# An attention and mixture-of-experts layer: one-hot token lists and gathers by token in place of a sorted copy of the rows

## The chip, the cores and the metric

The kernel runs on 1 core of one Trainium2 chip. The metric is the device time of one execution in microseconds; the median of 3 runs of the kernel before is 584.5 us (583.47 to 586.1). A page and a trace of one profiled execution go with it; that execution took 583.73 us.

## The reference

Two sublayers on x of 16 x 112 = 1792 tokens of 256 numbers, all in float32:

```
x = x + attention(layernorm(x), ctx, mask)       # 16 heads of 16, 375 context rows
flat = layernorm(x)                               # 1792 x 256
probs = softmax(flat @ router_w)                  # 8 experts
w, idx = top_k(probs, 2);  w = w / sum(w)
h = silu(einsum('td,edf->etf', flat, w1))         # w1: 8 x 256 x 512
y = einsum('etf,efd->etd', h, w2)                 # w2: 8 x 512 x 256
x = x + einsum('td,te->td', y, cw)                # cw: w of the two chosen experts, else 0
```

Only two of eight experts count for a token, so both kernels compute 1792 x 2 = 3584 rows of expert work and not 8 x 1792.

## The kernel before, in words

Each engine has its own instruction stream, written out by hand, and they meet at semaphores. Matmuls take operands in a rounded format (float32r); to keep float32 accuracy every operand is split in a high part and a low part (raw minus high), and a product is three matmuls (high x high, low x high, high x low).

**Attention** (lines 346 to 355, 721 to 745, 942 to 958, 1281 to 1383) is untouched by the change but for a few instructions on GpSimd behind line 554. It ends at about 310 us of the span.

**Residual, second norm, routing.** `project_output` (PE) and `residual` (DVE) make x2, 14 tiles of 128 tokens; `all_rstd` and `normalise_rows` make xn2, its layer norm. `flat_transpose`, `route` and `logits_back` give the logits, tokens on partitions. `find_first` and `find_second` (DVE, lines 1028 to 1046) mark the two chosen experts of each token in 0/1 tiles of 128 x 14 x 8. `rank` (PE, 1420) counts with a triangular matrix how many earlier tokens chose the same expert. `place_rows` (DVE, 1048) turns that into the place of each of the 3584 rows in a list sorted by expert, where each expert starts at a multiple of 256 (`TG`); `plan_steps` (1070) lists the expert of each of the 21 steps (`STEPS`), `weigh` (1078) the two weights of each token.

**Dispatch.** SyncE has filled `sorted_x`, a DRAM tensor of 21 x 256 rows, with zeros (line 420). When the places are known GpSimd scatters the rows of xn2 into it by 28 indirect DMAs of 128 rows (line 587). SyncE waits for all of them (461) before it loads the first block of rows.

**Experts**, 21 steps of 256 sorted rows, software pipelined; a hardware loop (`Fori`) runs steps 3 on in pairs. In turn t PE does `hidden(t)` (24 matmuls of 256 columns), `rows_transpose(t+1)` (4 transposes), `expert_out(t-1)` (24 matmuls). ScalarE: `w1_high(t+1)`, the write of y to `sorted_y` in DRAM, `rows_high(t+1)`, `silu(t)` (two passes). VectorE: `rows_low(t+1)`, `h_low(t)`, `copy_y(t-1)`, `w2_high(t+1)`. GpSimd: the low parts of w1 and w2 (line 592). SyncE loads w1, w2 (512 KB each) and 256 rows per step. Buffers are double.

**Combine.** When every step's y is in `sorted_y`, GpSimd gathers it back by token, 28 indirect DMAs of 128 rows (line 614); VectorE multiplies by the weight and adds to x2 (line 1165); SyncE writes out in 7 DMAs (473).

## Time and profile before

| | |
|---|---|
| median of 3 runs | 584.5 us (583.47 to 586.1) |
| profiled execution | 583.73 us, its span 582.0 us |
| busy in the span | PE 434.5, weight loads 383.9, VectorE 375.2, ScalarE 231.3, GpSimd 263.9 us |
| mean granted clock of TensorE | 0.873 |
| DMA | 93.00 MB, 160 GB/s |

The same in 40 slices of 14.55 us, each digit the busy share in tenths:

```
PE   3557799999999999999987472005999999998000
DVE  3765657777777777777735855001999999996233
ACT  3321235555555555555561130002545545553000
POOL 7352412222222222222006003774798999895574
PEclk9787769999999999999998685556999999999655
DMA  8979499999999999997245502426678878862354
```

PE is TensorE, DVE VectorE, ACT ScalarE, POOL GpSimd. Slices 0 to 20 are attention, 21 to 23 the second norm and the routing, 24 to 26 the dispatch, 27 to 36 the experts, 37 to 39 the combine.

### The profile page before, as it was taken

Reading aid. Unit: us, or ns where it says so; the run is one execution under the profiler, and the core shown is the slowest. Engines: PE = TensorE matmul, PEld = TensorE weight load, DVE = VectorE, ACT = ScalarE, POOL = GpSimd, SP = SyncE. Lnnn points to the kernel's source line nnn. Section 1 sums busy time; section 2 is a strip of 40 time slices with the busy share of each in tenths; the row PEclk is TensorE's granted clock in tenths of the full one; section 3 lists DMA queues with packets and bytes.
Section 4 is the critical chain, followed back from the end, with each engine's and each line's share of the span. In section 5 each row is a group of like instructions: output and inputs, shape, how many; then the busy total and the mean of one; then the engine's idle time right before and its main releaser. Section 6 shows DMA issues by size and latency. Waiting matters only on the chain.

```text
span 582.0 us, 10906 instructions
## 1 busy us (share of the span) xinstructions
PE 434.5 (75%) x4123; PEld 383.9 (66%) x4123; DVE 375.2 (64%) x733; ACT 231.3 (40%) x296; POOL 263.9 (45%) x170
## 2 busy tenths in 40 slices
PE   3557799999999999999987472005999999998000
PEld 2445588888888888888767462004999999998000
DVE  3765657777777777777735855001999999996233
ACT  3321235555555555555561130002545545553000
POOL 7352412222222222222006003774798999895574
PEclk9787769999999999999998685556999999999655
DMA  8979499999999999997245502426678878862354
GB/s 187 188 187 243 166 146 124 145 144 144 146 143 147 146 143 147 144 148 104 34 129 179 201 1 82 170 99 193 192 232 260 239 250 246 241 214 91 108 155 133
DMA packets 82504, 93.00 MB, mean 160 GB/s; under 512 B 19824, under 2 KB 75280, under 8 KB 82464
## 3 DMA queue, kind: packets, MB, share of 16 engines
q1 hardware_dynamic: 74064, 79.61, 64.6%
q0 software_dynamic: 2688, 7.34, 3.9%
q10 hardware_dynamic: 5712, 5.51, 2.8%
q8 instruction: 27, 0.44, 0.4%
q14 instruction: 13, 0.11, 0.1%
HBM read 51.58 MB, written 22.14 MB: 127 GB/s over the span
## 4 chain that ended last, share of the span: by engine, by line
PE 46%; issue 21%; DVE 14%; ACT 8%; POOL 5%; DMA 3%; ACTq 2%; SPq 1%; DVEq 0%; POOLq 0%
PE ps L1178 17%; PE ps L1228 10%; PE ps L1243 7%; PE ps L1257 7%; POOL chosen_rows L614 4%; ACT h_hi L775 3%; ACT h_f L774 2%; DVE y_out L1112 2%; DVE k_f L827 2%; ACTq L779 1%; DVE neg_max L843 1%; PE ps L1270 1%; DVE h_lo L1105 1%; DVE x_rows_sb L890 1%; PE ps L1399 1%
## 5 line engine op out<-in xcount | busy, mean ns | idle before, releaser
L843 DVE TENSOR_REDUCE neg_max<-ps 112x1 f32<-112x376 f32 x256 | 132.8, 545 | 48.7 <-PE ps L1228 44.8
L592 POOL TENSOR_TENSOR w_lo<-w_raw,w_hi 128x1024 fp32r<-128x1024 f32 x42 | 117.8, 2824 | 24.1 <-DVE w_hi L1101 14.3
L664 ACT ACTIVATE probs<-ps 125x1344 f32<-125x1344 f32 x64 | 82.7, 1292 | 59.2 <-PE ps L1243 56.4
L1228 PE MATMUL ps<-k_stack,q_stack 98*112 98x376 f32 x256 | 90.8, 396 | 10.5 <-issue 5.7
L502 POOL TENSOR_TENSOR k_lo<-k_f,k_hi 128x752 fp32r<-128x752 f32 x16 | 28.7, 1792 | 83.0 <-ACT k_hi L638 80.5
L493 POOL TENSOR_TENSOR ctx_lo<-ctx_raw,ctx_hi 128x752 fp32r<-128x752 f32 x16 | 28.8, 1799 | 79.2 <-ACT ctx_hi L631 79.2
L1228 PEld LDWEIGHTS ps<-k_stack,q_stack 98*112 98x112 f32 x256 | 42.9, 183 | 28.6 <-DVE neg_max L843 21.0
L1105 DVE TENSOR_TENSOR h_lo<-h_f,h_hi 128x1024 fp32r<-128x1024 f32 x21 | 52.6, 2503 | 11.1 <-ACT h_hi L775 11.1
L1243 PE MATMUL ps<-q_stack,k_stack 100*125 100x224 f32 x384 | 54.8, 279 | 2.1 <-ACT probs L664 1.3
L1243 PEld LDWEIGHTS ps<-q_stack,k_stack 100*125 100x125 f32 x384 | 51.2, 193 | 2.8 <-ACT probs L664 1.8
L1178 PE MATMUL ps<-flat_t_hi,w_hi 128*128 128x256 f32 x168 | 50.4, 300 | 3.4 <-DVE flat_t_lo L1094 3.1
L1257 PE MATMUL ps<-probs,v_wide 125*32 125x112 f32 x1536 | 50.6, 265 | 0.7 <-ACT probs L664 0.7
L1178 PE MATMUL ps<-w_hi,h_hi 128*128 128x256 f32 x168 | 49.1, 293 | 1.9 <-DVE h_lo L1105 1.9
L758 ACT CAST flat_t_hi<-ps 128x512 fp32r<-128x512 f32 x21 | 12.3, 587 | 94.6 <-PE ps L1438 94.6
L1178 PE MATMUL ps<-flat_t_hi,w_lo 128*128 128x256 f32 x168 | 48.1, 286 | 0.0
L1178 PE MATMUL ps<-flat_t_lo,w_hi 128*128 128x256 f32 x168 | 48.0, 286 | 0.0
L1178 PE MATMUL ps<-w_lo,h_hi 128*128 128x256 f32 x168 | 47.4, 282 | 0.0
L587 POOL DMA_INDIRECT sorted_x<-xn,place x28 | 27.1, 969 | 44.6 <-DVE place L1067 36.3
L1178 PE MATMUL ps<-w_hi,h_lo 128*128 128x256 f32 x168 | 47.3, 282 | 0.0
L1438 PE MATMUL ps<-ident,rows 128*128 128x128 f32 x84 | 13.1, 280 | 43.5 <-DMA rows<-sorted_x 43.5
L1101 DVE CAST w_hi<-w_raw 128x1024 fp32r<-128x1024 f32 x21 | 45.3, 2157 | 0.0
L1257 PEld LDWEIGHTS ps<-probs,v_wide 125*32 125x32 f32 x1536 | 35.0, 110 | 13.2 <-issue 11.8
(168 smaller groups left out, 986.0 us busy)
## 6 DMA issues: line engine op xcount, KB each, us to landing
w_raw<-w SPq DMA_DIRECT2D x42, 512.0 KB, 3.9
k_stack<-k_hi SPq DMA_DIRECT2D x64, 188.0 KB, 6.3
k_stack<-k_lo SPq DMA_DIRECT2D x32, 188.0 KB, 9.0
ctx_raw<-ctx_t SPq DMA_DIRECT2D x32, 187.5 KB, 9.1
q_stack<-q_scratch SPq DMA_DIRECT2D x32, 168.0 KB
sorted_x<-zeros SPq DMA_DIRECT2D x1, 5376.0 KB, 17.5
rows<-sorted_x SPq DMA_DIRECT2D x21, 256.0 KB, 4.0
sorted_y<-y_out ACTq DMA_DIRECT2D x21, 256.0 KB, 3.0
```

Source lines behind the costliest of these rows:

```text
L493: pool.tensor_tensor(cl[b.par][:, :, :], c_raw[b.par][:, :, :], ch[b.par][:, :, :].bitcast(F32), ALU.subtract).then_inc(cl_ready, 1)
L502: pool.tensor_tensor(kl[:, :, :], kf[:, :, :], kh[:, :, :].bitcast(F32), ALU.subtract)\
L587: pool.indirect_dma_start(sorted_x, bass.IndirectOffsetOnAxis(ap=place[c][:, n:n + 1], axis=0), xn2[:, n, :], None).then_inc(scattered, 16)
L592: pool.tensor_tensor(low[t.par][:, :, :], raw[:, :, :], high[t.par][:, :, :].bitcast(F32), ALU.subtract).then_inc(done, 1)
L664: act.activation(pf[j % 2][:, :, :], ps[0:CT, BK_ST:BK_ST + KT, 0:4 * S], ACT.Exp).then_inc(pf_ready, 1)
L843: dve.tensor_reduce(neg_max[:, s:s + 1], ps[0:S, BK_MAX + s % 2, 0:CP], AX.X, ALU.max, negate=True).then_inc(max_read, 1)
L1101: dve.tensor_copy(w2h[t.par][:, :, :], w_raw[t.par][1][:, :, :]).then_inc(w2h_ready, 1)
L1105: dve.tensor_tensor(hl[t.par][:, :, :], hf[t.par][:, :, :], hh[t.par][:, :, :].bitcast(F32), ALU.subtract).then_inc(hl_ready, 1)
L1178: last = pe.matmul(o, lhs, rhs, start=n == 0, stop=n == len(terms) - 1)
L1228: pe.matmul(ps[0:S, BK_MAX + a, 0:CP], qs[b.ring][0:R_MAX, q, S * a:S * (a + 1)], ks[b.ring][0:R_MAX, q, :], start=True, stop=True).then_i ...
L1243: last = pe.matmul(ps[0:CT, BK_ST + k3, 2 * S * q:2 * S * (q + 1)], ks[b.ring][0:ROWS, 2 * j + q, k3 * CT:(k3 + 1) * CT], qs[b.ring][0:ROW ...
L1257: last = pe.matmul(ps[VC * i:VC * (i + 1), BK_OUT, S * j:S * (j + 1)], vx[b.par][:, k3, 2 * j + i // 2 + HALF * (i % 2), :], pf[j % 2][:, ...
```

## The change

What it does:

- No sorted copies. xn2 is written to DRAM in token order (`xn_rows`), x2 as the start of the sum (`total`), each with 256 spare rows behind the 1792 real ones; in `xn_rows` and `total` these start as zeros.
- VectorE computes block (`place >> 7`) and place within the block of each row. It makes a 0/1 tile `is_place` (two choices x 14 tiles x 128 columns) and `block_token` (42 columns: token number + 1 where the row lies in that block). PE multiplies them, 28 matmuls added up, so that column b of the result holds the tokens of sorted block b on 128 partitions (`list_rows`). A second set of 28 matmuls does it with the weights, split in high and low, 84 columns. Empty rows get a spare row's number (`list_tokens`).
- Each step GpSimd gathers its 256 rows from `xn_rows` by two indirect DMAs, three steps ahead (three row buffers). VectorE multiplies y by the row's weight as it leaves PSUM (`weigh_y`); GpSimd adds the rows to `total` by two indirect DMAs that accumulate in DRAM, each step's pair only after the pair before has landed (two rows of one token can lie in different steps).
- The low parts of w1 and w2 go from GpSimd to VectorE, the high part of w2 from VectorE to ScalarE; ScalarE no longer writes y.
- `weigh` runs before `place_rows`, `plan_steps` after the first 14 one-hot tiles. The loops are written out, there is no `Fori`.
- At the end SyncE copies `total` to the output in one DMA from DRAM to DRAM.

The core of the diff:

```
@@ SyncE
-            sp.dma_start(sorted_x..., zeros...).then_inc(zero_rows, 16)
+            for rows_of, done in ((xn_rows, xn_written), (total, total_written)):
+                sp.dma_start(rows_of[T:TP, :]..., zeros...).then_inc(done, 16)
+            for g in range(NTG):
+                sp.wait_ge(resid_added, g + 1)
+                sp.dma_start(token_rows(total, g), x2[:, 2 * g:2 * g + 2, :]).then_inc(total_written, 16)
+            for g in range(NTG):
+                sp.wait_ge(xn2_ready, g + 1)
+                sp.dma_start(token_rows(xn_rows, g), xn2[:, 2 * g:2 * g + 2, :]).then_inc(xn_written, 16)
...
-            sp.wait_ge(scattered, 16 * TOP * NT)
-            load_block(zeroth)
...
+            sp.wait_ge(y_added, 16 * 2 * STEPS)
+            sp.dma_start(out, total[0:T, :].rearrange("(n p) d -> n p d", p=P)).then_inc(out_written, 16)
@@ GpSimd
-            (28 scatters, split_low of w1 and w2 each step, 28 gathers)
+            pool.iota(numbers_i ...) x4;  pool.tensor_copy(numbers[:, :], numbers_i[:, :])   # behind line 554
+            def gather_rows(t):
+                if early(t, 1):
+                    pool.wait_ge(xn_written, 16 * (NTG + 1))
+                    pool.wait_ge(list_ready, 1)
+                if not early(t, RINGS):
+                    pool.wait_ge(rt_done, t.n - RINGS + 1)
+                for a in range(2):
+                    pool.indirect_dma_start(rows[t.ring][:, a, :], None, xn_rows, token_of(t, a))...
+            def add_rows(t):
+                pool.wait_ge(y_copied, 2 * (t.n + 1))
+                if early(t, 1):
+                    pool.wait_ge(total_written, 16 * (NTG + 1))
+                else:
+                    pool.wait_ge(y_added, 16 * 2 * t.n)
+                for a in range(2):
+                    pool.indirect_dma_start(total, token_of(t, a), yo[t.par][:, a, :], None, compute_op=ALU.add)...
+            for n in range(-RINGS, STEPS + 1):
+                t = Batch(0, n)
+                if is_step(t.after(RINGS)):
+                    gather_rows(t.after(RINGS))
+                if is_step(t.after(-1)):
+                    add_rows(t.after(-1))
@@ ScalarE step(t):  w1_high(t+1), rows_high(t+1), silu(t), w2_high(t)
@@ VectorE
+            def weigh_y(t):
+                if early(t, 1):
+                    list_weights()
+                dve.wait_ge(y_done, t.n + 1)
+                if not early(t, 2):
+                    dve.wait_ge(y_added, 16 * 2 * (t.n - 1))
+                for a in range(2):
+                    dve.tensor_scalar(yo[t.par][:, a, :], ps[:, BK_Y + t.par, D * a:D * (a + 1)],
+                                      row_weight[:, 2 * t.n + a:2 * t.n + a + 1], None, ALU.mult)...
             def expert_step(t):
+                split_low w1(t+1);  rows_low(t+1)
+                weigh_y(t-1)
+                h_low(t);  split_low w2(t)
...
             find_first()
             find_second()
+            weigh()
             place_rows()
+            token_blocks()
+            places_in_block(0, 0)
+            places_in_block(0, 1)
             plan_steps()
-            weigh()
+            places_in_block(1, 0)
+            places_in_block(1, 1)
+            weight_blocks(0)
+            list_tokens()
+            weight_blocks(1)
@@ TensorE
             rank()
+            list_rows()
```

`token_blocks` is two products over 128 x 1176, `places_in_block` one comparison over 128 x 896, `weight_blocks` one product over 128 x 1176.

## Rows read from the trace of the kernel before

**Rows 1.** Windows: start:end, length, busy per engine, PEclk, DMA share, GB/s.
```profile
357.00:397.00 40.00, 0.30 (x2) 0.31 (x3) 3.89 (x15) 1.04 (x1) 29.48 (x29) 0.50 0.42 145
415.00:455.00 40.00, 39.93 (x330) 39.11 (x329) 37.81 (x27) 20.16 (x24) 36.23 (x13) 1.00 0.80 244
540.00:582.00 42.00, 0.00 (x0) 0.00 (x0) 13.56 (x28) 0.00 (x0) 26.63 (x28) 0.54 0.46 137
```

**Rows 2.** Timeline (start us, us, ...), routing to first expert step.
```profile
349.47 0.28 DVE L1044 TENSOR_TENSOR both_experts<-gate,gate 128x112 fp32r<-128x112 f32 x1
350.13 3.10 PE L1428 MATMUL ps<-both_experts,ones 128*128 128x112 f32 x14
355.25 0.27 DVE L1065 TENSOR_TENSOR gate<-gate,gate 128x112 f32<-128x112 f32 x1
356.55 0.17 DVE L1067 CAST place<-gate_col 128x14 int32<-128x14 f32 x1
...
358.50 0.34 DVE L1083 TENSOR_TENSOR gate<-gate,both_experts 128x112 f32<-128x112 f32 x1
358.53 0.97 POOL L587 DMA_INDIRECT sorted_x<-xn,place  x1 [0.30 <-issue]
...
362.85 1.04 ACT L765 CAST w_hi<-w_raw 128x1024 fp32r<-128x1024 f32 x1 [16.03 <-DMA w_raw<-w]
391.42 0.96 POOL L587 DMA_INDIRECT sorted_x<-xn,place  x1 [0.30 <-issue]
396.70 1.12 PE L1438 MATMUL ps<-ident,rows 128*128 128x128 f32 x4 [43.47 <-DMA rows<-sorted_x]
399.28 0.58 PE L1178 MATMUL ps<-flat_t_hi,w_hi 128*128 128x256 f32 x1 [1.47 <-DVE flat_t_lo L1094]
```

**Rows 3.** Groups of 415:535, shapes apart: busy us, mean ns, idle before.
```profile
L592 POOL TENSOR_TENSOR w_lo<-w_raw,w_hi 128x1024 fp32r<-128x1024 f32 x37 | 105.7, 2875 | 13.7 <-DVE w_hi L1101 13.7
L1112 DVE COPY y_out<-ps 128x512 f32<-128x512 f32 x19 | 12.9, 678 | 0.0
```

**Rows 4.** Lines L1105 and L904: duration ns min/median/max, first and last start.
```profile
L1105 DVE TENSOR_TENSOR h_lo<-h_f,h_hi x21: 1224/2576/3025, 408.4 to 533.7; 128x1024 fp32r<-128x1024 f32 x21
L904 DVE TENSOR_SCALAR q_f<-ps,bq_c x8: 669/674/684, 24.8 to 58.7; 128x448 f32<-128x448 f32 x8
```

**Rows 5.** Timeline of PE: first and last matmul of one `expert_out`.
```profile
454.61 0.36 PE L1178 MATMUL ps<-w_hi,h_hi 128*128 128x256 f32 x1
457.42 0.28 PE L1178 MATMUL ps<-w_hi,h_lo 128*128 128x256 f32 x1
```

**Rows 6.** Chain of waits (start us, us, what): one point two steps apart.
```profile
449.63 1.03 ACT h_f L774
...
462.37 1.03 ACT h_f L774
```

**Rows 7.** Timeline, the last step and the combine.
```profile
535.38 0.38 PE L1178 MATMUL ps<-w_hi,h_hi 128*128 128x256 f32 x1 [1.61 <-DVE h_lo L1105]
538.55 0.69 DVE L1112 COPY y_out<-ps 128x512 f32<-128x512 f32 x1 [2.63 <-PE ps L1178]
541.70 0.98 POOL L614 DMA_INDIRECT chosen_rows<-sorted_y,place  x1 [7.46 <-DMA sorted_y<-y_out]
542.99 0.96 POOL L614 DMA_INDIRECT chosen_rows<-sorted_y,place  x1 [0.30 <-issue]
545.74 1.00 DVE L1165 SCALAR_TENSOR_TENSOR x<-chosen_rows,weight,x 128x256 f32<-128x256 f32 x2 [6.49 <-DMA chosen_rows<-sorted_y,place]
579.44 0.37 SPq L473 DMA_DIRECT2D out<-x  x1
```

**Rows 8.** DMA issues (KB each, us to landing): the page, then 415:535, then 357:397.
```profile
sorted_x<-zeros SPq DMA_DIRECT2D x1, 5376.0 KB, 17.5
...
rows<-sorted_x SPq DMA_DIRECT2D x16, 256.0 KB, 4.0
...
rows<-sorted_x SPq DMA_DIRECT2D x2, 256.0 KB, 3.1
```

More of the change, by code:

```diff
@@ L451, in step @@
                     load_w1(t.after(2))
-                    load_block(t.after(2))
                 if is_step(t.after(1)):
@@ L581, in _ @@
                                    ALU.add).then_inc(xb_ready, 1)
-            pool.wait_ge(placed, 1)
-            pool.wait_ge(zero_rows, 16)
-            for n in range(NT):
-                for c in range(TOP):
-                    pool.indirect_dma_start(sorted_x, bass.IndirectOffsetOnAxis(ap=place[c][:, n:n + 1], axis=0),
-                                            xn2[:, n, :], None).then_inc(scattered, 16)
-            def split_low(t, raw, high, low, ready, done):
-                pool.wait_ge(ready, t.n + 1)
-                pool.tensor_tensor(low[t.par][:, :, :], raw[:, :, :], high[t.par][:, :, :].bitcast(F32),
-                                   ALU.subtract).then_inc(done, 1)
@@ new lines, in gather_rows @@
+            def gather_rows(t):
[5 more added lines that the diff above has]
+                for a in range(2):
+                    pool.indirect_dma_start(rows[t.ring][:, a, :], None, xn_rows, token_of(t, a))\
+                        .then_inc(rows_in[t.ring], 16)
+            def add_rows(t):
[5 more added lines that the diff above has]
+                for a in range(2):
+                    pool.indirect_dma_start(total, token_of(t, a), yo[t.par][:, a, :], None, compute_op=ALU.add)\
+                        .then_inc(y_added, 16)
@@ L1063, in place_rows @@
                                        ALU.add))
-                for one_of, c, dst in ((picked, c0, place[0]), (second, c1, place[1])):
-                    step(dve.tensor_tensor(t1[:, :, :], t0[:, :, :], one_of[:, :, :], ALU.mult))
-                    step(dve.tensor_reduce(c[:, :], t1[:, :, :], AX.X, ALU.add))
-                    last = dve.tensor_copy(dst[:, :], c[:, :])
-                last.then_inc(placed, 1)
+                step(dve.tensor_tensor(of_chosen[:, :, :, :], each_choice(t0), chosen[:, :, :, :], ALU.mult))
@@ new lines, in place_rows @@
+                step(dve.tensor_reduce(place[:, :, :], of_chosen[:, :, :, :], AX.X, ALU.add))
+                step(dve.tensor_copy(place_i[:, :, :], place[:, :, :]))
+                step(dve.tensor_scalar(block_i[:, :, :], place_i[:, :, :], 7, None, ALU.logical_shift_right))
+                step(dve.tensor_copy(block_of[:, :, :], block_i[:, :, :]))
+                step(dve.scalar_tensor_tensor(out=in_block[:, :, :], in0=block_of[:, :, :], scalar=-float(P),
+                                              in1=place[:, :, :], op0=ALU.mult, op1=ALU.add))
@@ new lines, in places_in_block, with weight_blocks @@
+            def places_in_block(c, half):
+                tiles = slice(HALF_NT * half, HALF_NT * (half + 1))
+                dve.tensor_tensor(is_place[:, c, tiles, :],
+                                  in_block[:, c, tiles].rearrange("p (n a) -> p n a", a=1).to_broadcast([P, HALF_NT, P]),
+                                  place_no.rearrange("p (n a) -> p n a", n=1).to_broadcast([P, HALF_NT, P]),
+                                  ALU.is_equal).then_inc(places_ready, 1)
+            def weight_blocks(part):
+                dve.tensor_tensor(block_weight[:, :, :, part, :], is_its_block[:, :, :, :],
+                                  by_block((weight_hi, weight_lo)[part]).bitcast(F32), ALU.mult)\
+                    .then_inc(weight_blocks_ready, 1)
@@ new lines, in list_tokens @@
+            def list_tokens():
+                dve.wait_ge(tokens_listed, 1)
+                listed = ps[:, BK_TOKEN, 0:NB]
+                step(dve.scalar_tensor_tensor(out=spare[:, :], in0=listed, scalar=0.0, in1=spare_no,
+                                              op0=ALU.is_equal, op1=ALU.mult))
+                dve.scalar_tensor_tensor(out=token_i[:, :], in0=listed, scalar=-1.0, in1=spare[:, :],
+                                         op0=ALU.add, op1=ALU.add).then_inc(list_ready, 1)
@@ L1070, in plan_steps, with list_weights @@
+            def list_weights():
+                dve.wait_ge(weights_listed, 1)
+                step(dve.tensor_copy(row_weight_lo[:, :], ps[:, BK_WEIGHT, NB:2 * NB]))
+                step(dve.tensor_tensor(row_weight[:, :], ps[:, BK_WEIGHT, 0:NB], row_weight_lo[:, :], ALU.add))
             def plan_steps():
+                step(dve.scalar_tensor_tensor(out=block_end[:, :], in0=first_row[:, :], scalar=1.0 / TG, in1=blocks[:, :],
+                                              op0=ALU.mult, op1=ALU.add))
@@ L1490, in _ @@
             rank()
-            for n in range(-1, 3):
-                step(Batch(0, n))
-            with pe.Fori(0, LOOP_STEPS) as i:
-                for off in (3, 4):
-                    step(Batch(i, off))
-            for n in range(3 + 2 * LOOP_STEPS, STEPS + 1):
+            list_rows()
+            for n in range(-1, STEPS + 1):
                 step(Batch(0, n))
```

257 lines of the change are left out of this document (130 added, 127 removed).

## The prediction, made before the changed kernel ran

> **What bounds the kernel now.** I read the page's 40 slices first. The reader is to see two holes there in which PE stands at 0: slices 25 and 26, and 37 to 39. Then the windows over them. In 357 to 397 us PE is busy 0.30 us and POOL 29.48; in 540 to 582 PE does nothing and POOL is busy 26.63 [rows 1]. Between them, 415 to 455, PE is busy 39.93 of 40 at clock 1.00 [rows 1]. So there are three regimes, each with its own bound.
>
> Dispatch: the places are known at 356.72 and the first expert transpose starts at 396.70 [rows 2]. In between POOL issues 28 indirect DMAs, 0.97 busy and 0.30 to the next, 1.26 each (358.53 to 391.42 is 26 pitches). PE's idle time there, 43.47, ended by the rows' DMA.
>
> Experts: two steps take 12.74 us (449.63 to 462.37 [rows 6]), one 6.37. The 24 matmuls of an `expert_out` start between 454.61 and 457.42, 0.12 us apart [rows 5]; 48 such, 4 transposes of the same pace and three joints of up to 0.2 fill the 6.37. It is PE bound, though DVE and POOL look nearly as busy.
>
> Combine: the last y is copied at 539.24, the first gather starts at 541.70, 28 gathers at 1.25 us follow, the last output write is issued at 579.44 [rows 7].
>
> **The change, part by part.** Attention: four iotas and a copy of 240 columns on POOL near 71 us. What waits behind them is one key split whose DMA SP issues 2.6 us after it is done. I take 0; at most some 1.5 us.
>
> Before 349.75: writes of 3.7 MB go out beside PE and DVE work, in place of the 5376 KB of zeros [rows 8]. 0.
>
> *Head.* Both choices are ready at 349.75 in either kernel [rows 2]. A DVE operation costs here 0.157 us + 1 column per 0.96 ns (0.27 for 112 columns), and 0.035 to the next. `weigh` took 2.5 us for its 8 common steps; with two operations of 224 columns (0.42 each) and two tiny ones it is 3.8, beside `rank` on PE (350.13 + 3.10 = 353.23 [rows 2]). So `place_rows` starts at 353.6, 0.3 later. It has eleven operations, 3.0 us: 356.6. `token_blocks`: 2 x 1.40 = 359.4. `places_in_block`: 1.12 each, two by 361.6. `plan_steps` 1.3: 362.9. Two more: 365.1. `weight_blocks(0)` 1.4: 366.5.
>
> PE's 28 small matmuls: the nearest row is `rank`, 14 in 3.10 us, 0.22 each whatever the columns (8 to 112), at half clock; at full clock the pace is 0.12. I take 0.22, since PE idles before. Tokens: seven per tile group at 360.5, 362.1, 364.0, 365.6, done at 367.3. `list_tokens` 0.5: the list at 367.9. Two gathers: the second is issued 1.25 later and lands 2.75 behind its issue (542.99 to 545.74 [rows 7]): rows at 372.
>
> But PE must first do the weights' list. `weight_blocks(1)` ends at 369.3, then 28 x 0.22 = 6.2: 375.6. So PE, not the gather, is late next. The weights of step 0: the table is 5.2 us later than before, w1 lands at 368, its low part is done by 370.6; hidden. The first transpose at 375.6 and `hidden(0)` 2.58 behind it as before [rows 2]: 378.2 against 399.28. **Head: -21.1.**
>
> *Steps.* Per step DVE has three splits of 128 x 1024 (1.22 each without POOL beside them, the minimum of L1105 [rows 4]; 2.58 is its median beside POOL's split), `rows_low` of 512 columns 0.68 like the copy of y [rows 3], and two `weigh_y` of 256 columns from PSUM: the nearest row is 0.67 for 448 columns, so 0.45 each, 0.85 with overlap. Sum 5.2. ACT has two casts of 1.04 [rows 2], two silus of 1.03 [rows 6] and 0.6: 4.7. POOL has four indirect issues, 5.0. None of the sums reaches 6.37.
>
> The chain does. `weigh_y(t-2)` can't start before y(t-2), and `h_low(t-1)` and the w2 split stand behind it on DVE, and `expert_out(t-1)` waits for that split. 0.08 + 0.85 + 1.22 + 1.22 + 0.06 = 3.43 us, then expert_out takes 3.09 (454.61 to 457.70 [rows 5]): a cycle of 6.52. PE needs 6.37. I take **6.5 a step**: 20 x 0.15 = +3.0. Filling the pipe costs 1.1 more (the w2 split, one 1.22 instruction, now stands before `expert_out(0)`), the end 1.9 more: h is done at 530.8 and `expert_out(20)` starts 4.6 later now [rows 7], with the new order (silu, wait for y(19), weigh, two splits) 6.5. **Steps: 139.2 + 6.0 = 145.2**, so the last y at 523.4.
>
> An accumulating DMA has no row. From below it is a plain one, 2.75 behind its issue [rows 7]; from above a read and then a write in a loaded queue: 2.75 x 4.0/3.1 (the rows' load beside and without the stream [rows 8]) x 2 = 7.1. I take 3.5. The pair then takes 1.25 + 3.5 = 4.75, under 6.5, so it does not set the pace. The DMA engines: 0.80 of 6.37 is 5.1 us a step; if the adds read as well as write, 5.9. Still under 6.5.
>
> *Tail.* y 523.4, weigh 0.95, first issue, second 1.25 later, landing 3.5: 529.2. The copy of 1792 KB from DRAM to DRAM has no row: the zeros' 307 GB/s gives 6.0, twice that 12, with its fixed part 8 to 14; I take 10. With issue and end 0.7: 539.9. **Tail: 43.5 before, 16.5 after, -27.0.**
>
> Sum: 582.0 - 21.1 + 6.0 - 27.0 = 539.9. The profiled execution lies 1.7 above its span, and the median 0.8 above that: **542 us**.
>
> **A rule against it.** At 358.50 a DVE product with two SBUF inputs took 0.34 beside an indirect issue (358.53), where its like at 355.25 took 0.27 without one [rows 2]: a cost of 0.07. Two splits on DVE and POOL at once took 2.58 and 2.88 instead of 1.22 [rows 3, 4]. The Trainium skill (SBUF — State Buffer, "Who interferes with whom") says that a VectorE instruction with two SBUF inputs and a GpSimd one that reads SBUF exclude one another for the whole instruction, and infers that descriptor generation is mostly spared. By its strict form the first rival below holds; by the 0.07 of the trace the sum stands.
>
> **Rivals.**
> (1) *POOL sets the pace.* Each step has four indirect issues on POOL and 3.7 us of two-input work on DVE. If each issue is held by half a split (0.6), POOL takes 4 x 1.86 = 7.4 a step, `weigh_y` waits for the adds, PE for DVE: +0.9 x 20 = +18, 560 us. For it: all three splits are now where POOL's reads can meet them. Against: 0.07 above. Nearly the same time comes if the add pair takes 1.25 + 6.
> (2) *Slower than before: the chain of adds.* Each pair waits until the one before has landed. At the upper bound the pair takes 1.25 + 7.1 + 0.35 = 8.7 us; then 20 x 2.2 = +44: 586. It decides only above 6.5 us a pair, and loses all the gain at 8.6. Against: gathers of the same size land in 2.75, and the read of 128 KB more is little work.
> (3) *The list is no bound and the clock helps*: if PE's clock rises during the 56 small matmuls, 0.12 each saves 3 us and up to 2 in the first step; a copy at the lower bound saves 2; DVE hides the 0.15. 535.
> (4) *The copy is slow*, a third of the rate of the zeros, as reads and writes of DRAM meet: 20 us in place of 10, 552. For the copy the Trainium skill (DMA: Bandwidth & Descriptors, "Rules for kernel authors") adds that an outermost dimension under 16, here 14, keeps a DMA to at most so many engines; 14/16 alone would cost 1 us, within the term.
>
> **Chances.** Forecast within 537 to 549: 0.48. (1) 0.22, (3) 0.12, (4) 0.10, (2) 0.05, rest 0.03. The time holds 8 in 10 between 532 and 568: (3) with the copy's lower end, (1) with part of (4). Faster by over 0.5% (which is about what a measurement tells from none) in all but (2): 0.94; same 0.01, slower 0.05.
>
> **What would show it.** Right: PE's hole after `rank` ends near 376, its first half with 28 small matmuls; L1105's median falls from 2.58 to about 1.3; steps of 6.4 to 6.6 with DVE's w2 split as what releases `expert_out`; the add pair landing within 6 us; 16 us from the last matmul to the end. Wrong: steps of 7 or more with DVE waiting in `weigh_y` for `y_added` (rivals 1, 2; the time of an indirect issue, 0.95 or more, tells them apart), a first transpose that waits for its rows, a copy of over 14 us.

## The result, and the profile after

The median of the changed kernel is 578.12 us (574.54 to 580.28), that of the kernel before beside it 584.18 us (583.47 to 586.1): ratio 0.989, interval 0.986 to 0.992. It is 1% faster where 7% was forecast, and outside the range of 532 to 568. The profiled execution took 580.28 us, the slowest of the four runs, its span 578.6; the forecast of the span was 539.9, so 38.7 us have to be found.

The windows over the changed kernel's dispatch and experts, answering to [rows 1]:

```profile
349.00:376.00 27.00, 16.91 (x75) 16.16 (x75) 17.99 (x41) 1.85 (x3) 6.77 (x7) 0.50 0.39 125
440.00:480.00 40.00, 31.78 (x234) 30.00 (x235) 23.13 (x28) 19.63 (x24) 26.75 (x19) 0.91 0.62 164
```

The hole of the dispatch is gone. In its place PE now has holes in the experts: 31.78 busy of 40 where the kernel before had 39.93 [rows 1], though VectorE, ScalarE and GpSimd each have 13 us or more to spare there. The timeline of the head of the changed kernel, answering to [rows 2] (of every timeline and chain here only the rows that the reading needs are shown):

```profile
359.65 6.26 PE L1491 MATMUL ps<-block_token,is_place 128*128 128x42 f32 x28 [7.11 <-DVE is_place L1098]
366.19 0.20 DVE L1114 SCALAR_TENSOR_TENSOR token_of_row<-ps,spare 128x42 int32<-128x42 f32 x1
367.28 1.45 POOL L612 DMA_INDIRECT rows<-xn_rows,token_of_row  x1 [47.03 <-DVE token_of_row L1114]
367.74 6.20 PE L1496 MATMUL ps<-block_weight,is_place 128*128 128x84 f32 x28 [1.82 <-DVE block_weight L1104]
374.05 1.12 PE L1507 MATMUL ps<-ident,rows 128*128 128x128 f32 x4
376.56 0.58 PE L1230 MATMUL ps<-flat_t_hi,w_hi 128*128 128x256 f32 x1 [1.40 <-issue]
```

The first transpose starts at 374.05 (396.70 in [rows 2]) right behind the second list, `hidden(0)` at 376.56. The end of the changed kernel, answering to [rows 7], and its copy in the list of DMA issues:

```profile
564.69 1.55 POOL L622 DMA_INDIRECT total<-y_out,token_of_row  x1 [2.81 <-DMA total<-y_out,token_of_row]
566.55 1.56 POOL L622 DMA_INDIRECT total<-y_out,token_of_row  x1 [0.30 <-issue]
570.25 0.62 SPq L485 DMA_DIRECT2D out<-total  x1
...
out<-total SPq DMA_DIRECT2D x1, 1792.0 KB, 7.9
```

From the last pair's first issue to the end of the span are 13.9 us; the forecast had 15.6 (539.9 less 523.4 and 0.95). So head and tail came as forecast or a little better, and everything missing lies between 376.56 and 564.69: 188.1 us, forecast 146.2. Between the first issues of successive pairs of adds are 8.57 us on average (393.2 to 564.69, 20 intervals), where the step was forecast at 6.5. The last three intervals, when the loads are over, are 6.2 to 6.9; the seventeen before them are 8.9 on average. This is the chain of waits of the changed kernel from 439 us on (start, us, what), answering to [rows 6]:

```profile
439.41 1.62 POOL total L622
441.03 0.30 issue
441.33 5.54 DMA total<-y_out,token_of_row
...
446.98 0.49 DVE y_out L1170
447.47 0.18 issue
447.65 1.62 POOL total L622
449.27 0.30 issue
449.57 6.02 DMA total<-y_out,token_of_row
...
456.36 1.62 POOL total L622
...
458.28 7.34 DMA total<-y_out,token_of_row
```

The adding DMAs and their issues fill it; the chain of the kernel before ran over ScalarE's `h_f` at this point [rows 6]. Read one link: an adding DMA is issued (1.62), the second of the pair follows 0.30 later, it lands 5.54, 6.02, 7.34 us behind the start of its issue (its own issue is inside that), and 0.73 to 0.77 after the landing GpSimd issues the next (446.88 to 447.65, 563.96 to 564.69). Each step's pair waits for the pair before it, so this chain closes on itself: 1.62 + 0.30 + 5.5 to 7.3 + 0.75 = 8.2 to 10.0. VectorE's `y_out` stands in it only because it waits for the same landing (its buffer is freed by it) and is done before GpSimd has come through its own 0.75; GpSimd starts as late where the chain has no `y_out` (landing at 473.80, issue at 474.57). The longest waits of 400 to 530 us of the changed kernel show what hangs on it (us in all, times, longest):

```profile
DVE y_out L1170 <- DMA total<-y_out,token_of_row: 45.0, 12, 5.2
...
PE ps L1507 <- DMA rows<-xn_rows,token_of_row: 16.3, 11, 3.1
```

and two of its groups, answering to [rows 3] and [rows 4]:

```profile
L622 POOL DMA_INDIRECT total<-y_out,token_of_row x30 | 55.2, 1840 | 37.0 <-DVE y_out L1170 28.4 <-issue 4.6 <-DMA total<-y_out,token_of_row 4.1
...
L1155 DVE TENSOR_TENSOR w_lo<-w_raw,w_hi 128x1024 fp32r<-128x1024 f32 x32 | 37.6, 1217 | 0.0
...
L1160 DVE TENSOR_TENSOR h_lo<-h_f,h_hi 128x1024 fp32r<-128x1024 f32 x16 | 19.4, 1214 | 0.0
```

The low part of h did fall from 2.58 [rows 4] to 1.21 us, as forecast, and those of w1 and w2 take 1.22 on VectorE where GpSimd took 2.88 [rows 3]. The adding issue is the new price: 1.84 us on average here, where a plain one is 0.97 [rows 2].

### The profile page after: what moved, and what is told of

The parts are those of the page before. It is cut to its first block, busy times and chain, and to the rows that moved or that the text cites. A ratio compares the mean times of both kernels' runs of the same rounds, so it can differ in the third digit from the quotient of the medians.

```text
span 578.6 us, 10708 instructions
## 1 busy us (share of the span) xinstructions
PE 460.2 (80%) x4179; PEld 407.5 (70%) x4179; DVE 352.7 (61%) x757; ACT 251.1 (43%) x317; POOL 214.0 (37%) x161
## 3 DMA queue, kind: packets, MB, share of 16 engines
q0 software_dynamic: 8064, 11.02, 10.2%
## 4 chain that ended last, share of the span: by engine, by line
PE 51%; DMA 19%; DVE 12%; issue 7%; POOL 7%; ACT 2%; POOLq 0%; SPq 0%; DVEq 0%
PE ps L1230 21%; DMA total<-y_out,token_of_row 16%; PE ps L1280 10%; PE ps L1295 7%; PE ps L1309 7%; POOL total L622 5%; DMA rows<-xn_rows,token_of_row 2%; DVE k_f L836 2%; DVE y_out L1170 1%; PE ps L1322 1%; DVE neg_max L852 1%; PE ps L1491 1%; DVE x_rows_sb L899 1%; PE ps L1451 1%; ACT probs L678 1%
## 5 line engine op out<-in xcount | busy, mean ns | idle before, releaser
L622 POOL DMA_INDIRECT total<-y_out,token_of_row x42 | 77.1, 1836 | 62.9 <-DVE y_out L1170 45.1
L612 POOL DMA_INDIRECT rows<-xn_rows,token_of_row x42 | 43.5, 1035 | 64.4 <-DVE token_of_row L1114 47.0
L1230 PE MATMUL ps<-w_hi,h_hi 128*128 128x256 f32 x168 | 54.2, 323 | 16.1 <-issue 14.4
L1170 DVE TENSOR_SCALAR y_out<-ps,weight_of_row 128x256 f32<-128x256 f32 x42 | 18.4, 479 | 73.5 <-DMA total<-y_out,token_of_row 53.3
L1280 PEld LDWEIGHTS ps<-k_stack,q_stack 98*112 98x112 f32 x256 | 43.1, 183 | 27.9 <-DVE neg_max L852 21.2
L1230 PE MATMUL ps<-w_lo,h_hi 128*128 128x256 f32 x168 | 52.2, 311 | 0.0
L1230 PE MATMUL ps<-w_hi,h_lo 128*128 128x256 f32 x168 | 52.2, 311 | 0.0
L1230 PEld LDWEIGHTS ps<-w_hi,h_hi 128*128 128x128 f32 x168 | 37.3, 222 | 19.9 <-issue 19.9
L1230 PE MATMUL ps<-flat_t_hi,w_hi 128*128 128x256 f32 x168 | 48.9, 291 | 2.8 <-issue 1.4
L1155 DVE TENSOR_TENSOR w_lo<-w_raw,w_hi 128x1024 fp32r<-128x1024 f32 x42 | 49.6, 1217 | 0.3 <-issue 0.3
```

The costliest lines, as they stand in the source:

```text
L612: pool.indirect_dma_start(rows[t.ring][:, a, :], None, xn_rows, token_of(t, a))\
L622: pool.indirect_dma_start(total, token_of(t, a), yo[t.par][:, a, :], None, compute_op=ALU.add)\
L1155: dve.tensor_tensor(low[t.par][:, :, :], raw[:, :, :], high[t.par][:, :, :].bitcast(F32), ALU.subtract).then_inc(done, 1)
L1170: dve.tensor_scalar(yo[t.par][:, a, :], ps[:, BK_Y + t.par, D * a:D * (a + 1)], row_weight[:, 2 * t.n + a:2 * t.n + a + 1], None, ALU.mult ...
L1230: last = pe.matmul(o, lhs, rhs, start=n == 0, stop=n == len(terms) - 1)
L1280: pe.matmul(ps[0:S, BK_MAX + a, 0:CP], qs[b.ring][0:R_MAX, q, S * a:S * (a + 1)], ks[b.ring][0:R_MAX, q, :], start=True, stop=True).then_i ...
```

## The experiments

"Cycle" is the mean time between the first issues of successive pairs of adds over all 21 steps (in v1, v2 and p1 of the writes of y; in h1 there are none), in us. Ratios are against the kernel before, run beside each, with the 95% interval. Every run but e3, h1, v1, v2 and p1 leaves a part of the work out or does it wrongly, as its text says, and serves only to find the bound.

| kernel | median us (range) | ratio | cycle |
|---|---|---|---|
| before | 583.2 to 585.4 (four medians) | 1 | |
| changed | 578.12 (574.54–580.28) | 0.989 (0.986–0.992) | 8.57 |
| e1_plain_scatter | 539.35 (539.14–539.57) | 0.923 (0.920–0.926) | 6.57 |
| e2_two_sums | 548.81 (547.89–549.73) | 0.939 (0.936–0.943) | 7.15 |
| e3_three_yo | 564.31 (562.79–569.42) | 0.968 (0.961–0.974) | 7.90 |
| e4_weights_once | 556.24 (554.45–558.03) | 0.952 (0.947–0.957) | 7.37 |
| h1_head_only | 562.85 (560.85–564.14) | 0.964 (0.959–0.968) | |
| v1_own_rows | 547.91 (547.13–549.89) | 0.939 (0.935–0.943) | 6.45 |
| p1_low_on_pool | 641.40 (640.31–642.49) | 1.098 (1.093–1.104) | 11.07 |
| e5_three_yo_weights_once | 564.45 (562.91–565.98) | 0.967 (0.962–0.972) | 7.68 |
| e6_tiny_splits | 581.42 (578.77–584.81) | 0.996 (0.993–0.998) | 8.72 |
| e7_tiny_splits_weights_once | 542.64 (542.16–543.12) | 0.929 (0.926–0.931) | 6.68 |
| e8_tiny_splits_two_sums | 539.18 (537.19–541.17) | 0.923 (0.918–0.927) | 6.37 |
| v2_rows_before_weights | 548.01 (547.24–549.17) | 0.937 (0.936–0.939) | 6.47 |
| e9_half_loads | 557.22 (557.03–557.41) | 0.952 (0.946–0.958) | 7.39 |
| e10_three_yo_tiny_splits | 557.60 (556.34–558.86) | 0.953 (0.941–0.964) | 7.50 |
| e11_gathers_once | 577.48 (577.36–577.59) | 0.987 (0.980–0.993) | 8.46 |

### Is it the adding?

The same DMA, at the same place, waited for in the same way, but it writes its rows and does not add:

```diff
-  pool.indirect_dma_start(total, token_of(t, a), yo[t.par][:, a, :], None, compute_op=ALU.add)
+  pool.indirect_dma_start(total, token_of(t, a), yo[t.par][:, a, :], None)
```

> The changed kernel with plain indirect writes where it has accumulating ones; the wait of each pair for the one before stays. The sum is left out: a row keeps the last y written. Theory (chain of adds): a step takes 0.77 us from a landing to the next issue, 1.92 between the two issues, and 5.5 to 7.3 from the second issue to its landing, 8.6 in the mean. If the read-modify-write is what makes the landing long, it falls to 3 to 4 us, the issue to 0.95 + 0.30, the pair to about 6, and the steps to the 6.4 to 6.6 of PE: 533 to 540 us. Rival (the weights' stream is what delays any DMA of the software queue): the landing stays at 5 to 6 us, a step at 7.5 or more, 560 to 575 us.

539.35 us, as the chain theory expected: 38.8 less than the changed kernel, the whole of what was missing, and the span of 537.4 lies 2.5 under the forecast's 539.9. The cycle is 6.57, forecast 6.5. So the sum's other terms stand within a few us, and the adding costs 38.8 us, by its issue, its landing, or both. The rival is not empty: most pairs of plain writes follow one another in 6.1 to 6.7 us, but single ones land late beside the loads as well (5.11 us behind the issue at 431.12, a pair of 7.19).

### Is it that each pair waits for the one before?

Even and odd steps add to two tensors, so a pair waits only for the pair two steps back:

```diff
-  pool.wait_ge(y_added, 16 * 2 * t.n)
-  ...(total, token_of(t, a), yo[t.par][:, a, :], None, compute_op=ALU.add).then_inc(y_added, 16)
+  pool.wait_ge(y_sum[t.par], 32 * t.turn)
+  ...((total, total_odd)[t.par], token_of(t, a), yo[t.par][:, a, :], None, compute_op=ALU.add).then_inc(y_sum[t.par], 16)
```

> The changed kernel with two sums in DRAM, one for even and one for odd steps, so that each pair of adds waits only for the pair two steps before. Only the even sum goes to the output. Chain theory: the wait has two steps of room, the bound is then POOL's four issues (1.6 + 2.0 + 2 x 1.0 and three gaps of 0.3, some 6 us) or PE: steps of 6.4 to 7, 535 to 548 us. Rival (accumulating DMAs are limited by the DMA engines' rate, not by their order): steps stay near 8.6 and the time near 578.

548.81 us, just above the 535 to 548 expected (the terms named there add up to 6.5, not to "some 6"): 29.3 of the 38.8 come back. The rest is another bound. The groups of GpSimd in 400 to 500 us of this kernel:

```profile
L626 POOL DMA_INDIRECT total<-y_out,token_of_row x14 | 26.9, 1923 | 4.3 <-issue 4.3
...
L616 POOL DMA_INDIRECT rows<-xn_rows,token_of_row x26 | 31.1, 1196 | 7.9 <-issue 7.6 <-PE ps L1511 0.3
```

GpSimd waits for next to nothing but its own 0.3 between issues: 2 x 1.92 + 2 x 1.20 + 4 x 0.3 = 7.4, and the cycle in this window is 7.4 (7.15 over all steps, since the last ones are shorter). With the chain opened, GpSimd sets the pace.

### More room for y

Three buffers for y instead of two: VectorE no longer waits for the pair before in order to weigh.

```diff
-  yo = [sb(f"y_out{p}", [P, 2, D]) for p in range(2)]
+  yo = [sb(f"y_out{p}", [P, 2, D]) for p in range(RINGS)]
-  dve.wait_ge(y_added, 16 * 2 * (t.n - 1))
+  dve.wait_ge(y_added, 16 * 2 * (t.n - 2))
```

> The changed kernel with three y buffers in place of two, so that VectorE never stands in weigh_y for the adds. Rival (VectorE is blocked by the buffer, as the table of waits says with 45 us of y_out waiting for the adds, and holds h_low and the split behind it): the steps come near 6.5 to 7, 540 to 550 us. Chain theory: the pace is set by the adds alone, VectorE's wait is a consequence; the time stays within 1% of the changed kernel's 578.

564.31 us, 14 less than the changed kernel: both expectations missed. The pairs still follow one another one by one, yet the cycle fell to 7.90. A closed chain of issue and landing can only get shorter if its links do, so the landing had to depend on what VectorE releases. That was open here.

### The weights' loads

w1 and w2 are loaded for steps 0 and 1 only, all steps use them:

```diff
-  if is_step(t.after(2)): load_w1(t.after(2))
-  if is_step(t.after(1)): load_w2(t.after(1))
+  if t.n == 0: load_w2(t.after(1))
```

> The changed kernel with the weights loaded for steps 0 and 1 only and used by all (the wrong experts' weights from step 2 on); the adds as they are. If the weights' stream (1 MB a step) is what stretches the landing from the 3.6 to 4.3 us of the last steps to 5.5 to 7.3, the pair falls to 6.7 and the time to 540 to 545 us. If the read-modify-write is slow by itself, the landing stays above 5 and the time above 565.

556.24 us, between the two expectations. The landing of an add is 4.0 us in the median without the loads, so they do lengthen it; but the adds' issues stayed at 1.85 us in the mean: the first of each pair at 1.62, the second, beside VectorE's splits, mostly at 1.9 to 2.3. Both edits at once, that of e3 and that of e4:

> Both loosenings of the chain at once: three y buffers and the weights loaded for steps 0 and 1 only (wrong experts' weights from step 2 on). Alone they gave 564 and 556 against the changed kernel's 578. If both act only by the same thing (the weights' loads fall into the adds' flight time because VectorE's splits release both at once), the second adds little to the first: 550 to 556. If the two are separate (buffer wait and queue sharing), they add up: the bare chain of 6.2 to 6.9 us a pair, 540 to 546.

564.45 us, slower than the loads' removal alone (556.24), which neither expectation had. The timeline of e5, rows of VectorE and GpSimd:

```profile
440.67 0.88 DVE L1168 TENSOR_SCALAR y_out<-ps,weight_of_row 128x256 f32<-128x256 f32 x2 [3.05 <-DMA total<-y_out,token_of_row]
441.46 1.22 DVE L1158 TENSOR_TENSOR h_lo<-h_f,h_hi 128x1024 fp32r<-128x1024 f32 x1
441.56 2.61 POOL L620 DMA_INDIRECT total<-y_out,token_of_row  x1 [0.44 <-DVE y_out L1168]
442.59 2.36 DVE L1153 TENSOR_TENSOR w_lo<-w_raw,w_hi 128x1024 fp32r<-128x1024 f32 x2
444.48 1.92 POOL L620 DMA_INDIRECT total<-y_out,token_of_row  x1 [0.30 <-issue]
```

An adding issue that meets VectorE's splits takes 2.61 us instead of 1.62, and with three buffers it is often the first of the pair that meets them. In 400 to 500 us the adds' mean is 2.01 and the gathers' 1.28, so GpSimd needs 2 x 2.01 + 2 x 1.28 + 1.2 = 7.8 a step, and the cycle there is 7.9 (7.68 over all steps). Rival 1 is a bound after all, hidden behind rival 2. The Trainium skill (SBUF — State Buffer, "Who interferes with whom") has the splits exclude a GpSimd instruction that reads SBUF for their whole length, and infers that `tensor_tensor` spares descriptor generation. Here the hold is 1.0 us at the longest beside a split of 1.22, and 0.3 on average: nearer to the exclusion than to the inference, and the 0.07 on which I relied was a product of 112 columns.

### The same without the splits

To take that hold out, the splits of w1 and w2 on VectorE work on 8 columns of each block from step 2 on (128x16 and 128x32 in place of 128x1024), and the rest of the low parts is not renewed:

```diff
-  dve.tensor_tensor(low[t.par][:, :, :], raw[:, :, :], high[t.par][:, :, :].bitcast(F32), ALU.subtract)
+  w = slice(None) if early(t, 2) else slice(0, 8)
+  dve.tensor_tensor(low[t.par][:, :, w], raw[:, :, w], high[t.par][:, :, w].bitcast(F32), ALU.subtract)
```

> The changed kernel with VectorE's splits of w1 and w2 cut to 16 and 32 columns from step 2 on (the rest of the low parts is left as it was, so the products are less exact). It takes away the two-input work of VectorE beside GpSimd's issues; chain, loads and gathers stay. An adding issue takes 1.55 us at best and up to 2.6 beside a split. If that hold lies on the chain, it goes: by the means of 1.84 for an adding issue, 0.3 off each of two, steps of 8.0 and 564 to 568 us. If the chain is only landing time, under 1% off 578. If VectorE's own chain is what matters (weigh, h_low, split in a row behind the landing), 550 or less.

581.42 us, cycle 8.72: no gain, and under 1% off 578, as the landing theory expected. In the changed kernel the hold is not on the chain, though VectorE is now busy 32 of 100 us and adding issues are 1.57 to 1.62. What is left is landing time. With the loads taken away too (e4's edit on e6):

> As the run with the weights loaded for two steps only, 556 us and 7.4 us a step, and VectorE's splits cut as well: the chain of adds with next to nothing beside it. The last steps of the changed kernel, which have neither loads nor gathers beside them, take 6.2 to 6.9 us a pair. If loads and the hold by VectorE explain the rest, steps of 6.4 to 6.8 and 537 to 545 us; if the steps stay over 7.2, something else stretches them.

542.64 us, cycle 6.68, within the expected 537 to 545 and close to e1. The chain of waits of e7:

```profile
441.58 1.62 POOL total L620
443.20 0.30 issue
443.50 3.83 DMA total<-y_out,token_of_row
...
448.10 1.62 POOL total L620
...
450.02 3.70 DMA total<-y_out,token_of_row
```

Without the loads an adding DMA lands 3.7 to 3.8 us behind its issue, against 5.5 to 7.3 above. The chain is then 1.62 + 0.30 + 3.8 + 0.77 = 6.5, about PE's own pace (PE is busy 98 of 100 us). e6 and e7 differ in the loads alone, so the 2.0 us between their cycles are the least that the loads add to the landing. They do it to plain gathers too. DMA issues in 400 to 500 us, us to landing, median of both of a pair, first e6, then e7:

```profile
total<-y_out,token_of_row POOLq DMA_INDIRECT x22, 5.0
rows<-xn_rows,token_of_row POOLq DMA_INDIRECT x22, 4.4
...
total<-y_out,token_of_row POOLq DMA_INDIRECT x30, 3.8
rows<-xn_rows,token_of_row POOLq DMA_INDIRECT x30, 2.8
```

Without the loads an add lands 1.0 us later than a gather, 0.6 of it its longer issue; the loads add 1.2 to the adds' median and 1.6 to the gathers'. The gathers stand between the adds in GpSimd's order, so in the changed kernel they come late when the adds do, and PE's waits for rows (16.3 us above) hang on the same chain. And with the chain opened in place of the loads (e2's edit on e6):

> As the run with two sums (549 us, 7.15 us a step), with VectorE's splits cut. There the adds had room of two steps, so the bound should have been GpSimd itself: two adding issues of 1.88 and two gathers of 1.17 in the mean, four gaps of 0.3, 7.3 us. Without VectorE beside it: 2 x 1.55 + 2 x 0.97 + 1.2 = 6.2, under PE's 6.4: 532 to 537 us. If the accumulating DMAs' landing still bound it, no change.

539.18 us, cycle 6.37, PE's own pace, though above the expected 532 to 537. Its groups of GpSimd in 400 to 500 us:

```profile
L626 POOL DMA_INDIRECT total<-y_out,token_of_row x14 | 22.4, 1599 | 4.3 <-issue 4.0 <-DMA total_odd<-y_out,token_of_row 0.3
...
L616 POOL DMA_INDIRECT rows<-xn_rows,token_of_row x31 | 34.1, 1099 | 9.4 <-issue 9.1 <-DMA total<-y_out,token_of_row 0.3
```

Adds at 1.60 here and 1.92 in e2 show the splits' hold at work, worth 548.8 - 539.2 = 9.6 us once the chain is open. In this window GpSimd still needs 2 x 1.63 + 2 x 1.10 + 1.2 = 6.7 (1.63 the mean over both sums), and the cycle there is 6.7: it stays level with PE (busy 96 of 100) or just behind it, which the expected 6.2 left out.

### Which load, how much, and when

Half of the loads (e6, w1 loaded each step, w2 only for steps 0 and 1):

```diff
   if is_step(t.after(2)): load_w1(t.after(2))
-  if is_step(t.after(1)): load_w2(t.after(1))
+  if t.n == 0: load_w2(t.after(1))
```

> The changed kernel with VectorE's weight splits cut and w2 loaded for steps 0 and 1 only, w1 every step: half the bytes of the loads. With all loads a step takes 8.7 us, with none 6.7. If the loads stretch the landing in proportion to their bytes: 7.5 to 7.9 a step, 558 to 566 us. If only one of the two loads falls into the flight of the adds, the step is near one of the ends (under 7.2 or over 8.3).

557.22 us: cycles 8.72, 7.39, 6.68 with two, one and no loads of 512 KB a step. That is just under the 7.5 to 7.9 expected of a stretch in proportion to the bytes. The first load taken away gives 1.33, the second 0.71, and there the chain is already level with PE. Only w2's load was taken away alone, not w1's.

Gathers once (e6, rows gathered for steps 0 to 2 only):

```diff
-  if is_step(t.after(RINGS)): gather_rows(t.after(RINGS))
+  if t.n < 0: gather_rows(t.after(RINGS))
```

> The changed kernel with VectorE's weight splits cut and rows gathered for steps 0 to 2 only (later steps work on these rows), all loads and adds. If the gathers ahead of or behind the adds in GpSimd's queue stretch their landing, the step falls from 8.7 to 7.5 or less (under 560 us). If only the loads do, it stays over 8.3 (over 572).

577.48 us, cycle 8.46. The gathers, 256 KB a step on GpSimd's own queue, cost the chain 0.26 us a step; the 1024 KB that SyncE issues are the load, as expected.

Three buffers of y (e3's edit) on e6, to settle what e3 left open:

> Three y buffers and VectorE's weight splits cut, all loads. Three buffers alone gave 7.9 us a step and 564 us, cut splits alone 8.7 and 581. If three buffers help because loads and adds no longer start in one phase, the gain of 0.7 a step stays or grows when VectorE's hold on GpSimd goes: 7.2 to 7.8, 550 to 562 us. If the splits' length was what spread the loads, the gain is lost: 8.3 and more, 572 or more.

557.60 us, cycle 7.50 against 8.72 with the same loads, so the gain stays without the splits. First the timeline of e6, then that of e10, at the same point of a step:

```profile
439.00 1.62 POOL L622 DMA_INDIRECT total<-y_out,token_of_row  x1 [3.70 <-DVE y_out L1171]
440.25 0.27 DVE L1156 TENSOR_TENSOR w_lo<-w_raw,w_hi 128x32 fp32r<-128x32 f32 x2
440.61 1.82 SPq L463 DMA_DIRECT2D w_raw<-w  x2
440.92 1.57 POOL L622 DMA_INDIRECT total<-y_out,token_of_row  x1 [0.30 <-issue]
447.98 0.88 DVE L1171 TENSOR_SCALAR y_out<-ps,weight_of_row 128x256 f32<-128x256 f32 x2 [6.85 <-DMA total<-y_out,token_of_row]
448.65 1.62 POOL L622 DMA_INDIRECT total<-y_out,token_of_row  x1 [3.53 <-DVE y_out L1171]
```

```profile
438.46 1.56 SPq L463 DMA_DIRECT2D w_raw<-w  x2
439.35 1.62 POOL L622 DMA_INDIRECT total<-y_out,token_of_row  x1 [0.30 <-issue]
441.28 1.57 POOL L622 DMA_INDIRECT total<-y_out,token_of_row  x1 [0.30 <-issue]
446.29 1.62 POOL L622 DMA_INDIRECT total<-y_out,token_of_row  x1 [0.81 <-DMA total<-y_out,token_of_row]
```

With two buffers the landing of a pair lets VectorE weigh, the splits behind it free the raw buffers, and SyncE issues both loads (440.61) right before the second add (440.92): it lands about 7.0 us behind its issue. With three, the loads go out (438.46) 2.8 us before the second add (441.28), and it lands about 4.2 behind (5.01 to the next issue, less 0.8). The pair starts the loads that delay it. These two points are no exceptions. The landing of the second add can be read in each step as the next pair's issue less 0.77. In e6 from 410 to 525 us a load is issued 0.3 us before every second add, and these land in 5.8 to 7.2. In e10 from 400 to 510 us the five second adds with a load issued within 1.3 us, before or behind, land in 5.7 to 7.6, and the ten with no load nearer than 1.4 in 3.8 to 4.3. In the changed kernel from 410 to 530 us the load comes 0.7 to 1.1 us behind the second add (5.5 to 7.3), so it is the nearness and not the order that goes with the delay. No run moved the loads' issue by itself, and where in the DMA engines the add meets the loads is not seen in the rows. The Trainium skill (DMA: Bandwidth & Descriptors, "Issuing engines are not separate DMA queues") says that DMAs of all issuers run on the same engines and interleave; this case agrees, with GpSimd's adds slower by 1.8 to 3.6 us beside SyncE's loads.

### The head and the low parts alone

The kernel with the new dispatch and expert steps, but y unweighted to `sorted_y` and combined as before (28 gathers by `place`, VectorE's product and sum):

```diff
-  add_rows(t)                       # GpSimd
+  act.dma_start(sorted_y[TG * t.n:TG * (t.n + 1), :]..., yo[t.par][:, :, :])    # ScalarE
...
+  pool.indirect_dma_start(y_of[c][:, n, :], None, sorted_y, IndirectOffsetOnAxis(ap=place_i[:, c, n:n + 1], axis=0))
```

> One part of the change alone: the token lists by one-hot products and the gathers per step, the low parts on VectorE as in the changed kernel, but y goes unweighted to a sorted copy by ScalarE's queue and is gathered at the end by 28 indirect DMAs, as before. By the prediction's terms: first expert matmul near 377, steps 139 plus 3 to 6, combine 43.5 as before: 565 to 570 us. If the gathers per step cost PE time of their own, steps of 7 or more and 575.

562.85 us, 20 less than the 583.2 of the kernel before beside it, 2 below the expectation. PE is busy 111.68 of 115 us at clock 1.00 in the steps (400 to 515 us), so the head's gain comes through nearly whole if no chain is added behind it.

### A version without the adding

Each row of y has a row of its own: 3584 for the two choices of each token, and one for each empty row of a step. So plain indirect writes do, and none waits for another but for the buffer. At the end SyncE loads both halves in token order (14 plain DMAs) and VectorE adds them to x2. The list's numbers carry the choice (token + 2048 x choice, 2048 being the 1792 rows and 256 spare ones), and `xn_rows` is written twice, so that the same number gathers the row.

```diff
-  pool.iota(... token numbers, pattern=[[P, NT]] ...)
+  pool.iota(... token numbers, pattern=[[TP, TOP], [P, NT]] ...)
-  pool.wait_ge(y_added, 16 * 2 * t.n)
-  pool.indirect_dma_start(total, token_of(t, a), yo[t.par][:, a, :], None, compute_op=ALU.add)
+  pool.indirect_dma_start(y_rows, token_out_of(t, a), yo[t.par][:, a, :], None)
...
+  sp.dma_start(y_of[c][:, 2 * g:2 * g + 2, :], token_rows(y_rows, c, g))
+  dve.tensor_tensor(x2, x2, y_of[0], ADD); dve.tensor_tensor(x2, x2, y_of[1], ADD)
```

> A kernel meant to beat both: the head and the steps of the changed one, but each of the two choices of a token has a row of its own in DRAM, so the weighted y is written by plain indirect DMAs and no pair waits for another. The sum is made at the end: plain loads of both rows of every token (3.7 MB), two adds on VectorE per group, seven output writes. By the run with plain writes (539) the steps take 6.5 to 6.6 us; the tail is some 6 us longer than there: loads 11 to 12, adds and last write 4, against one copy of 8. 543 to 549 us. Rival (the indirect writes beside the weights' stream stay slow in themselves): steps over 7, 556 us or more.

547.91 us, as expected: 35 less than the 583.2 of the kernel before beside it, 30 less than the changed kernel. Its windows over the steps and the tail:

```profile
400.00:515.00 115.00, 113.81 (x925) 110.46 (x924) 86.02 (x107) 75.45 (x88) 87.66 (x67) 1.00 0.68 229
520.00:545.00 25.00, 1.79 (x9) 1.50 (x8) 10.56 (x16) 0.00 (x0) 1.94 (x2) 0.57 0.71 231
```

PE is the bound (113.81 of 115); the writes of y are still issued in 0.96 to 1.97 us beside the splits and land in 4.0 in the median, but nobody waits. From the last issue of a write (524.25) to the end of its span are 21.2 us, 9 more than in the changed kernel (566.55 to 578.6), since 14 loads, 14 sums and 7 writes stand there.

The same with the low parts of w1 and w2 back on GpSimd (`split_low` moved from VectorE's step to GpSimd's):

```diff
@@ VectorE expert_step
-  split_low(after, w_raw[after.par][0], w1h, w1l, ...);  split_low(t, w_raw[t.par][1], w2h, w2l, ...)
@@ GpSimd, each turn
+  split_low(t.after(1), w_raw[...][0], w1h, w1l, ...)     # between the gathers and the writes
+  split_low(t, w_raw[t.par][1], w2h, w2l, ...)            # behind the writes
```

> The kernel with a row of its own per choice, but the low parts of w1 and w2 back on GpSimd beside its four indirect DMAs per step. GpSimd's work per step: two splits of 2.35 to 2.88 and four issues of 1.26, 9.8 to 10.8 us, over PE's 6.4. Theory: it sets the pace, +3.3 to 4.3 us a step, 610 to 635 us. Rival (moving the splits mattered little, since they only lengthen VectorE's chain): below 560.

641.40 us, 93 more than v1, worse than the 610 to 635 expected. In 400 to 600 us of this kernel:

```profile
400.00:600.00 200.00, 136.23 (x932) 129.72 (x932) 52.92 (x72) 78.65 (x91) 167.46 (x105) 0.89 0.41 135
...
L640 POOL TENSOR_TENSOR w_lo<-w_raw,w_hi 128x1024 fp32r<-128x1024 f32 x37 | 87.4, 2366 | 0.8
```

GpSimd is busy 167.46 of 200: two splits of 2.37 each beside four issues. A step of 11.07 is 9.3 of its work, 0.8 between issues and 1.0 of waiting for y; the last was not in the expected sum. The move of the splits to VectorE was not a detail but what lets GpSimd issue four indirect DMAs in a step of PE's length.

Last, v1 with `rows_transpose(0)` put between the halves of the weights' list, so that PE need not do all 28 matmuls first:

```diff
+  if (c, n) == (1, 0):
+      rows_transpose(Batch(0, 0))
```

> The kernel with a row of its own per choice (547.9), with the four transposes of the first step's rows put between the two halves of the weights' 28 small matmuls, so that ScalarE and VectorE split the rows while PE does the second half. The first expert matmul then follows the matmuls at once: 2.2 to 2.5 us earlier, 545.5 us. If PE stands there for the rows' landing, which is near, under 1 us.

548.01 us, no gain; the second half of the expectation holds. In its timeline PE waits 3.06 us for the rows at the transpose, which starts no earlier than in v1 (374.81):

```profile
375.15 1.11 PE L1533 MATMUL ps<-ident,rows 128*128 128x128 f32 x4 [3.06 <-DMA rows<-xn_rows,token_of_row]
```

The list and the gather are late at nearly the same time.

## Why the prediction was wrong

Right, by its own steps. *Bound before*: three regimes, as described; the dispatch's hole went with its own edit (h1), and where no chain was added the steps stayed PE's (h1, v1). *Head*: forecast 375.6 and 378.2, measured 374.05 and 376.56, about half of the 1.6 because the routing itself ended 0.7 to 0.9 earlier in this execution (one slip of writing there: "1 column per 0.96 ns" should be 0.96 columns per ns, which is what its terms use); the 28 matmuls took 6.26 and 6.20, forecast 6.2; PE was late next, as said. *Steps without the adding*: 6.5 forecast, 6.57 in e1. *Low parts*: 1.22 as forecast, and p1 shows what they cost on GpSimd beside four issues. *Tail*: the copy took 7.9 for a forecast of 10, just under its lower bound of 8, the tail 13.9 for 15.6.

Wrong is one term, the time of a pair of adds, where the prediction says "An accumulating DMA has no row … I take 3.5. The pair then takes 1.25 + 3.5 = 4.75, under 6.5, so it does not set the pace." Measured, the pair takes 8.57, 3.8 more:

- from the first to the second issue 1.92 where 1.25 was taken: the adding issue is 1.62 and not 0.95 (+0.67);
- the landing of the second 5.5 to 7.3 under the loads, 5.9 on average over all steps, and 3.7 to 3.8 without them (e7), where 3.5 was taken (+2.4): the value was nearly right without the loads, but in this kernel they are issued within about 1 us of it;
- 0.75 from the landing to the next issue, which the sum put at nothing (+0.75).

So the step that failed is "it does not set the pace": at 8.57 the chain of pairs sets it, 2.1 us a step above the 6.5 of VectorE and PE. Over 20 steps these are 41 us; the miss is 38.7 because head and tail came 3 us better.

This is rival (2), slower than before, with its mechanism as written: at its upper bound of 7.1 it had 8.7 a step. That the pace was right to 0.13 is partly luck: its landing was 1.2 too long, its issue and its way from landing to issue together 1.1 too short. Its 586 came out as 578 because the steps took 2.1 less than its sum, head and tail 3.3 less, and the median lies 0.5 under the profiled span where 2 above was reckoned. It had a chance of 0.05. What was weighed wrongly was the choice inside the bounds, 3.5 between 2.75 and 7.1, by the nearest row, which was a gather in an idle tail [rows 7]. For a chain that repeats in every step the row to stand nearest is the one under the same load: the rows' load takes 4.0 beside the stream [rows 8], and that is a plain load. The middle between this 4.0 and the upper bound of 7.1 is 5.5, an estimate that would have made a pair of 1.25 + 5.5 + 0.35 = 7.1, above 6.5, and rival (2) likely.

Rival (1), a pace set by GpSimd, has a true mechanism: VectorE's splits hold the issues. In the changed kernel it is hidden behind the slower chain (e6: no gain without it), and it decides as soon as that is opened (e2 against e8: 9.6 us). That e2's rows sum to the 7.4 that it named is luck in part: the mean hold is 0.3 and not 0.6 an add, and the rest is that an adding issue costs 0.65 more by itself. Rival (3) and rival (4) did not come.

Still open: how a DMA that adds spends the 3.7 us, and why its landing grows by more when a load is issued within about 1 us of it; no row here shows the parts. The split between read and write was not tried, nor loads held back until a pair has landed.

## What to carry to other kernels

A DMA on whose landing the next one waits is a chain with a pace of its own: issue + landing under the real load + the way from landing to issue, and it is that sum that has to be set against the step, with the landing taken from a row under the same traffic. If each result can have a place of its own, let the transfers be free of one another and add at the end: here that was worth 30 us, a tail 9 us longer already taken off. And when GpSimd issues DMAs, count VectorE's work on two SBUF inputs beside them as part of the issue.

## What the runs showed of the hardware

- An indirect DMA that adds is issued in 1.55 to 1.62 us, a plain one of the same 128 rows in 0.94 to 1.00, where VectorE's splits do not meet it. The queue of indirect DMAs has 2688 packets for 56 of them in the kernel before, 48 each, and 4032 in e1 for 84, again 48. In the changed kernel it has 8064 for 42 gathers and 42 adds: an add has 144. The bytes are the same 11.02 MB in both, the packets' time is 10.2% of the 16 DMA engines' span against 5.7% in e1.
- Without the loads the second add of a pair lands 3.7 to 3.9 us behind its issue in most steps (e7), with two loads of 512 KB a step 5.5 to 7.3 (changed kernel).
- A VectorE `tensor_tensor` of 1024 columns with two SBUF inputs holds GpSimd's issue: up to 1.97 us instead of 0.96 (v1), up to 2.61 instead of 1.62 (e5, and the changed kernel), 0.3 in the mean of e2 against e8.
- 0.73 to 0.77 us pass from the landing of a DMA to the start of the next indirect issue that waited for it.
- The copy of 1792 KB from DRAM to DRAM landed 7.9 us behind its issue, 232 GB/s.
